# FFN weight halves made in the steps of pairs 3 to 5, the low ones on GpSimd, instead of in pairs 6 to 13 on VectorE

## The reference

```python
mod = silu(c) @ wmod                         # sa, ca, ga, sb, cb, gb for each sequence
h = layernorm(x) * (1 + ca) + sa
x = x + ga * linear_attention_with_memory(h) # 32 dims, causal
h = layernorm(x) * (1 + cb) + sb
gate = softmax(h @ w_gate.T); top 2 of 8 experts, weighted by cw
y = gelu(h @ W1[e] + b1[e]) @ W2[e] + b2[e]  # W1: 8 x 128 x 512, W2: 8 x 512 x 128
x = x + gb * sum over experts of cw * y
```

## Time and profile before

| | |
|---|---|
| median of 3 runs | 492.51 us (491.37 to 492.91) |
| the profiled execution's own time | 490.82 us |
| its span, first to last instruction | 489.0 us |
| VectorE busy | 417.5 us (85%) |
| TensorE busy (matmul) | 342.1 us (70%) |
| ScalarE busy | 306.5 us (63%) |
| GpSimd busy | 304.6 us (62%) |

### The profile page before, as it was taken

The page is one execution under the profiler, slowest core; times in us unless marked ns, Lnnn a source line. Parts: engine busy times, 40 slices in busy tenths (PEclk is TensorE's granted clock), DMA queues, the critical chain, the costliest instruction groups (busy, mean ns, idle before and its releaser), DMA issues.

```text
span 489.0 us, 13386 instructions
## 1 busy us (share of the span) xinstructions
PE 342.1 (70%) x3736; PEld 303.2 (62%) x3737; DVE 417.5 (85%) x1078; ACT 306.5 (63%) x691; POOL 304.6 (62%) x360
## 2 busy tenths in 40 slices
PE   1673664738765785673389999999999999995000
PEld 1462564627664665562269989999999999984000
DVE  1879999889998889885759888989899898988997
ACT  1262483739993998373166676776767677669930
POOL 2208830037774776576777834888888888887760
PEclk9976766958985888587599999999999999999555
DMA  8895000002420333235165564666655665653653
GB/s 211 216 312 207 3 1 0 7 22 99 145 102 33 135 104 109 69 97 167 53 173 149 146 117 111 143 145 141 148 137 141 145 145 137 143 122 95 180 157 107
DMA packets 98774, 59.62 MB, mean 122 GB/s; under 512 B 45872, under 2 KB 92080, under 8 KB 98480
## 3 DMA queue, kind: packets, MB, share of 16 engines
q1 hardware_dynamic: 90544, 42.38, 31.3%
q0 software_dynamic: 8192, 16.79, 13.3%
HBM read 21.75 MB, written 23.10 MB: 92 GB/s over the span
## 4 chain that ended last, share of the span: by engine, by line
PE 47%; DVE 34%; issue 9%; ACT 7%; DVEq 1%; ACTq 1%; POOL 0%; POOLq 0%
PE psA L1296 20%; PE psA L1284 10%; PE psV L1284 5%; PE psH L1284 5%; DVE ATT L812 3%; DVE stats L751 2%; PE psH L1182 2%; DVE X L1107 2%; DVE X L888 2%; DVE w_parts L1021 2%; DVE stats L895 1%; ACT ATT L649 1%; DVE ROW L1104 1%; PE psA L1191 1%; PE psA L1193 1%
## 5 line engine op out<-in xcount | busy, mean ns | idle before, releaser
L536 POOL DMA_INDIRECT expert_rows<-ROW,POS x128 | 130.6, 1020 | 71.4 <-issue 37.2
L1296 PE MATMUL psA<-WST,ATT 128*128 x1704 | 114.0, 220 | 1.7 <-DVE ATT L1077 1.7
L1296 PEld LDWEIGHTS psA<-WST,ATT 128*128 128x128 f16 x1704 | 103.2, 98 | 8.9 <-issue 2.8
L1077 DVE SCALAR_TENSOR_TENSOR ATT<-ATT,f_scales 128x1024 f16<-128x1024 f32 x71 | 91.2, 1284 | 2.5
L551 POOL DMA_INDIRECT ROW<-expert_out,POS x64 | 69.3, 1083 | 29.9 <-issue 26.6
L694 ACT ACTIVATE ATT<-psA,b1T,f_scales 128x256 f32<-128x256 f32 x144 | 69.6, 563 | 27.4 <-PE psA L1284 27.0
L551 POOL DMA_INDIRECT BIG<-expert_out,POS x64 | 67.6, 1056 | 17.7 <-issue 15.9
L1075 DVE TENSOR_SCALAR ATT<-ATT,f_scales 128x1024 f16<-128x1024 f32 x71 | 53.8, 757 | 7.2 <-ACT ATT L694 2.1
L1284 PE MATMUL psA<-WT,WST 128*128 128x256 f16 x432 | 54.4, 277 | 3.1 <-ACT ATT L694 1.6
L694 ACT ACTIVATE ATT<-psV,b1T,f_scales 128x256 f32<-128x256 f32 x70 | 35.7, 561 | 30.7 <-PE psH L1284 30.7
L1182 PE MATMUL psH<-ident,ATT 128*128 128x128 f32 x64 | 14.7, 371 | 47.9 <-DVE ATT L812 47.9
(11 more groups left out here) (246 smaller groups left out, 757.1 us busy)
## 6 DMA issues: line engine op xcount, KB each, us to landing
expert_out<-VP SPq DMA_DIRECT2D x71, 128.0 KB
X<-in_x SPq DMA_DIRECT2D x8, 512.0 KB, 7.0
WST<-in_W SPq DMA_DIRECT2D x2, 2048.0 KB, 14.6
WST<-WT SPq DMA_DIRECT2D x16, 256.0 KB
out<-X SPq DMA_DIRECT2D x15, 256.0 KB, 2.3
expert_rows<-ROW,POS POOLq DMA_INDIRECT x128
GA<-gate_rows SPq DMA_DIRECT2D x1, 2048.0 KB, 10.1
GA<-gate_rows SPq DMA_DIRECT2D x1, 1792.0 KB, 10.9
```

Of the source, the lines that this page charges most:

```text
L536: nc.gpsimd.indirect_dma_start(xg, bass.IndirectOffsetOnAxis(ap=POS[:, k * TILES + t:k * TILES + t + 1], axis=0), ROW[:, t * 2 * D:(t + 1) ...
L1077: nc.vector.scalar_tensor_tensor(out=GL[:, k % 2, :], in0=G[:, k % 2, :], scalar=f_scales[:, 3:4], in1=GH[:, k % 2, :], op0=ALU.mult, op1= ...
L1296: last = mm(psD[k % 2][:, h * D:(h + 1) * D], a[:, k % 2, i:i + TOK], W2S[:, ds(e * 2 * FF + b * FF + m * D, D)], start=(m == 0 and c == 0 ...
```

## The change

The weights' magnitudes are reduced earlier (`first_bound` and `middle_bounds` after step 1, `last_bound` beside step 2), the scales follow after step 2, and the statistics of the first layer norm that stood there move one step later each. The high halves are made by ScalarE in steps 3, 4 and 5 (5, 5 and 6 chunks). GpSimd makes the low halves with two instructions a chunk: it scales the f32 chunk in place and subtracts the high half. The halves go to a ring of four chunks in the part of `ROW` that is not yet written (instead of two in `WT`); ScalarE waits before chunk c until chunk c-4 has been moved by DMA, and before `route(0)` until all are moved. SyncE issues the moves of chunks 0 to 8 after `MR` of pair 5, 9 to 13 after that of pair 6, 14 and 15 after that of pair 7. VectorE's low halves are gone.

```diff
@@ -48,6 +48,8 @@
+    WRING = 4
+    WSTEP = {3: range(0, 5), 4: range(5, 10), 5: range(10, 2 * E)}
@@ -163,7 +165,7 @@
-        WP = WT[:].bitcast(f16).rearrange("p (i c) -> p i c", i=2)
+        WP = ROW[:, TILES * D:TILES * D + WRING * 2 * FF].rearrange("p (i c) -> p i c", i=WRING)
@@ -264,14 +267,15 @@
             for p in range(-1, 6):
-                step(p, p % 2, p // 2, bisect(PAIRS_TO, p - 2), **({"beside": beside[p]} if p in beside else {}))
+                step(p, p % 2, p // 2, bisect(PAIRS_TO, p - 2), **({"beside": beside[p]} if p in beside else {}),
+                     **({"weights": WSTEP[p]} if weights and p in WSTEP else {}))
...
-                        step(2 * n + k, k, n, g + 1, **({"weights": (g, 2 * n - 6 + k)} if weights else {}))
+                        step(2 * n + k, k, n, g + 1)
@@ -406,10 +410,8 @@
             def move(c):
-                if 0 <= c < 2 * E:
-                    for i in range(2):
-                        sp.wait_ge(ws_low, c + i + 1)
-                        sp.dma_start(WCHUNKS[:, (c + i) * FF:(c + i + 1) * FF], WT[:, i * FF:(i + 1) * FF]).then_inc(ws_moved[i], 16)
+                sp.wait_ge(ws_low, c + 1)
+                sp.dma_start(WCHUNKS[:, c * FF:(c + 1) * FF].bitcast(f16), WP[:, c % WRING, :]).then_inc(ws_moved[c % WRING], 16)
@@ -418,10 +420,11 @@
                 sp.dma_start(MR[:, p % 2, :], MEMO[:, p, :]).then_inc(mr_in[p % 2], 16)
-                move(2 * (p - LOOPED - 3))
+                for c in {5: range(0, 9), 6: range(9, 14), 7: range(14, 2 * E)}.get(p, ()):
+                    move(c)
@@ -464,9 +467,6 @@
-            for i in range(2):
-                nc.gpsimd.memset(WP[:, i, 0:1], 0.0).then_inc(ws_moved[i], 16)
@@ -522,6 +522,14 @@
             nc.gpsimd.partition_all_reduce(w_bound_all[:, 0:3], w_bound[:, 0:3], 128, bass.bass_isa.ReduceOp.max).then_inc(wb_all, 1)
+            pool.wait_ge(ws_ready, 4)
+            for c in range(2 * E):
+                chunk = WCHUNKS[:, c * FF:(c + 1) * FF]
+                pool.wait_ge(ws_high, c + 1)
+                nc.gpsimd.tensor_scalar(chunk, chunk, f_scales[:, c // E:c // E + 1], None, ALU.mult).then_inc(ws_scaled, 1)
+                pool.wait_ge(ws_scaled, c + 1)
+                nc.gpsimd.tensor_tensor(WP[:, c % WRING, FF:2 * FF], chunk, WP[:, c % WRING, 0:FF], ALU.subtract).then_inc(ws_low, 1)
@@ -576,13 +584,11 @@
-            def weights_high(pair, n):
-                c = 2 * pair
-                for i in range(2):
-                    ge(act, ws_moved[i], 16 * (pair + 1))
...
+            def weights_high(c):
+                ge(act, ws_moved[c % WRING], 16 * (c // WRING))
+                nc.scalar.activation(WP[:, c % WRING, 0:FF], WCHUNKS[:, c * FF:(c + 1) * FF], ACT.Copy,
+                                     scale=f_scales[:, c // E:c // E + 1]).then_inc(ws_high, 1)
@@ -625,7 +631,8 @@
                     act.wait_ge(ws_ready, 4)
-                    weights_high(weights[1], weights[0])
+                    for c in weights:
+                        weights_high(c)
@@ -677,13 +684,16 @@
             def route(g):
+                if g == 0:
+                    for i in range(WRING):
+                        act.wait_ge(ws_moved[i], 16 * 2 * E // WRING)
...
-            steps(act, step, route, {0: lambda: first_norm(1), 2: lambda: first_norm(2), 4: lambda: act.wait_ge(ln1_ready, 3)},
+            steps(act, step, route, {0: lambda: first_norm(1), 3: lambda: first_norm(2)},
                   weights=True, last=last_rows)
@@ -811,15 +821,7 @@
-            def weights_low(c, n):
-                for i in range(2):
-                    ge(dve, ws_high, c + i + 1)
-                    nc.vector.scalar_tensor_tensor(out=WP[:, i, FF:2 * FF], in0=WCHUNKS[:, ds((c + i) * FF, FF)],
...
@@ -871,8 +873,6 @@
-                if weights is not None:
-                    weights_low(2 * weights[1], weights[0])
@@ -1057,16 +1057,18 @@
-            def bounds_and_tiles():
+            def scales_and_bounds():
                 scales()
+                first_bound()
+                middle_bounds()
+            def weights_and_tiles():
+                weight_scales()
                 tiles(LN1[2], SECOND_HALF)
-            def last_refine():
-                refine(2)
-                middle_bounds()
-            steps(dve, step, route, {0: second_statistics, 1: bounds_and_tiles, 2: lambda: statistics(2, SECOND_HALF + BESIDE), 3: last_refine, 4: weight_scales},
-                  weights=True, beside={2: lambda: tiles(SECOND_HALF, SECOND_HALF + BESIDE), 3: first_bound, 4: last_bound})
+            steps(dve, step, route, {0: second_statistics, 1: scales_and_bounds, 2: weights_and_tiles,
+                                     3: lambda: statistics(2, SECOND_HALF + BESIDE), 4: lambda: refine(2)},
+                  beside={2: last_bound, 3: lambda: tiles(SECOND_HALF, SECOND_HALF + BESIDE)})
```

More of the change, by code:

```diff
@@ L214, in build_adaln_block @@
         bnd_ready, bnd_all, wb_ready, wb_all = sem("bnd_ready"), sem("bnd_all"), sem("wb_ready"), sem("wb_all")
-        ws_ready, ws_high, ws_low, ws_moved = sem("ws_ready"), sem("ws_high"), sem("ws_low"), [sem(f"ws_moved{i}") for i in range(2)]
+        ws_ready, ws_high, ws_low, ws_moved = sem("ws_ready"), sem("ws_high"), sem("ws_low"), [sem(f"ws_moved{i}") for i in range(WRING)]
+        ws_scaled = sem("ws_scaled")
         xn_ready, xn_turned, hT_ready = sem("xn_ready"), sem("xn_turned"), sem("hT_ready")
@@ L420, in _ @@
                 sp.dma_start(MR[:, p % 2, :], MEMO[:, p, :]).then_inc(mr_in[p % 2], 16)
-                move(2 * (p - LOOPED - 3))
-            for i in range(2):
-                sp.wait_ge(ws_moved[i], 16 * (E + 1))
+                for c in {5: range(0, 9), 6: range(9, 14), 7: range(14, 2 * E)}.get(p, ()):
+                    move(c)
+            for i in range(WRING):
+                sp.wait_ge(ws_moved[i], 16 * 2 * E // WRING)
             sp.wait_ge(zeroed, 16)
@@ L578, in _ @@
             nc.scalar.activation(gate_terms[:, 0:1], gate[:], ACT.Exp, scale=-1.0).then_inc(g_exp, 1)
-            def weights_high(pair, n):
-                c = 2 * pair
-                for i in range(2):
-                    ge(act, ws_moved[i], 16 * (pair + 1))
-                    nc.scalar.activation(WP[:, i, 0:FF], WCHUNKS[:, ds((c + i) * FF, FF)], ACT.Copy,
-                                         scale=f_scales[:, n:n + 1]).then_inc(ws_high, 1)
+            def weights_high(c):
+                ge(act, ws_moved[c % WRING], 16 * (c // WRING))
+                nc.scalar.activation(WP[:, c % WRING, 0:FF], WCHUNKS[:, c * FF:(c + 1) * FF], ACT.Copy,
+                                     scale=f_scales[:, c // E:c // E + 1]).then_inc(ws_high, 1)
             def rows(s):
@@ L812, in norm, with step @@
                 return nc.vector.tensor_scalar(out, x, mean, rstd, ALU.subtract, ALU.mult)
-            def weights_low(c, n):
-                for i in range(2):
-                    ge(dve, ws_high, c + i + 1)
-                    nc.vector.scalar_tensor_tensor(out=WP[:, i, FF:2 * FF], in0=WCHUNKS[:, ds((c + i) * FF, FF)],
-                                                   scalar=f_scales[:, n:n + 1], in1=WP[:, i, 0:FF], op0=ALU.mult,
-                                                   op1=ALU.subtract).then_inc(ws_low, 1)
-            def step(p, j, half, g, weights=None, beside=None):
+            def step(p, j, half, g, beside=None):
                 q, r = p - 1, p - 2
@@ L1311, in turn_needs @@
                 mm(psQK[0:1, 0:CHUNKS], need_col[:], ident[:, 0:CHUNKS], start=True, stop=True).then_inc(need_turned, 1)
-            for i in range(2):
-                pe.wait_ge(ws_moved[i], 16 * (E + 1))
+            for i in range(WRING):
+                pe.wait_ge(ws_moved[i], 16 * 2 * E // WRING)
             pe.wait_ge(row_ready, PAIRS)
```

## The result

The changed kernel takes 523.41 us (median of 6 runs, 523.06 to 524.14), the kernel before 491.55 (6 runs, 491.24 to 492.91): a ratio of 1.064, 95% interval 1.0623 to 1.0657. The forecast was 518 us in a range of 505 to 524, so the sign was right and the time lies at the range's upper edge. The profiled execution of the changed kernel took 524.14 us, its span 522.3. In its lines 843 has become 845, 812 is 822, 584 is 590 and 642 is 649; 881 has kept its number.

A forecast was written before the change was run, and what follows sets the result against it. TensorE and VectorE hold most of the chain; attention steps are bound by VectorE, then the path from `XN2` to `HL`. 490.8 + 1.7 + 0.7 + 11.7 + 17.8 - 6.1 = 516.6, forecast 518 us as the median, range 505 to 524.

The forecast's parts named there:

- Data and scales: Before step 3: VectorE waits 1.7 us for `b2B`, loses 0.7 of cover, waits 11.7 at the scales for GpSimd.
- No second load: Rival: GpSimd's second reduction loads no code, so the scales' wait is 5.9 instead of 11.7; 512 us, chance 0.29.
- The ring: Steps 3 to 5 and `route(0)`: waits for chunks' return through GpSimd and DMA cost 17.8 us, at 2.1 a chunk.
- The shared port: Steps 3 to 5: GpSimd may delay VectorE's `XN2` by 2 us, covered by ScalarE's ring wait; zero in the sum.
- VectorE pays the port, or the scaling costs 1.26: Rival: GpSimd blocks VectorE beyond the ring's cover, or scaling makes a chunk 2.7 us; 522 to 528 us, chance 0.07.
- The gain: Steps 6 to 13: without weight work each falls from 9.56 to 8.80 us, 6.1 in all (4.6 to 10.6).
- Not slower: Rival: the experts' first slot doesn't move with the steps, so early waits vanish; 492 us or less, chance 0.04.
- ring hides all: Rival: a chunk and its DMA fit within three high halves (2 us), ScalarE never waits; 500 us, chance 0.05.
- The signs of being wrong: GpSimd at the magnitudes before 62 us, a chunk clearly under 2 us, or step 6 under 20 us later than 106.2.

The follow-up runs named there:

- experiment 1: Kernel before with only VectorE's order of the changed kernel (earlier reductions and scales); halves still made in steps 6 to 13: 506.37 us, ratio 1.0259.
- experiment 7: Changed kernel with one more reduction over partitions on GpSimd behind the last chunk, its result unread: 528.58 us, ratio 1.0718.
- experiment 6: Changed kernel with GpSimd's small operations on the cells moved behind chunk 4 instead of ahead of the second reduction: 519.7 us, ratio 1.0546.
- experiment 3: Kernel before with one added GpSimd product behind the second reduction over partitions, its result unread: 485.57 us, ratio 0.9853.
- experiment 8: Changed kernel with eight ring places, ScalarE's wait for all moves at route 1, low halves on VectorE, one tiny GpSimd product: 504.92 us, ratio 1.0235.
- experiment 4: Changed kernel with eight ring places instead of four and ScalarE's wait for all moves at route 1 instead of route 0: 509.07 us, ratio 1.0327.
- experiment 2: Kernel before without making the halves in steps 6 to 13; the 16 moves stay and carry zeros from a GpSimd memset: 490.88 us, ratio 0.9964.
- experiment 5: Changed kernel without GpSimd's scaling instruction, so a chunk there is the subtraction alone: 514.85 us, ratio 1.0435.

## Why the prediction was right, and where it was not

The forecast case named the right places for the losses: the data, the scales behind a second load, the ring in steps 3 to 5 and the route. It did not have the head and put the port at nothing, and its sum came out near partly by luck, because errors of both signs met. In the order of its terms:

**Data and scales (1.7, 0.7, 11.7).** Right for the old head: 13.9 for 14.1 us in experiment 1. The changed kernel starts 6.6 us earlier on VectorE, which then stands at 42.6 for the same data, so the data's wait becomes 7.28; GpSimd's cells end 5 us earlier (61.9), so the scales' wait becomes 7.12. The step that failed was to leave the head as it was: the added chunks make GpSimd end on other code than it did, a gain that no term held. Step 3 starts at 73.18 us, for 76.52 in experiment 7 and 79.70 in experiment 1, so it is worth 3.3 to 6.5 us there.

**No second load (0.29).** It falls: 5.94 us here, 6.12 in experiment 6, 5.76 in experiment 7. The Trainium skill, "GPSIMD Engine Reference", section 2.1, speaks of a load of about 6 us at the first call to a freshly loaded kernel; the rows agree if each change of code counts as fresh, for the same reduction pays it at each of its two calls.

**The ring (17.8).** Mis-sized: against the order alone, steps 3, 4, 5 and route 0 grew by 5.5, 6.3, 9.9 and 4.9, together 26.6. The chunk: 2.8 for 2.1, since the scaling takes 1.57 us and not 0.65. The estimate put an operation with one input below one with two; here it is above it (1.15). GpSimd starts chunk 0 at 75.95 although its high half ended at 74.9, where in step 4 it follows within 0.1 us; chunk 4 waits 4.34, chunk 9 only 3.35. A third load, back from the reduction's code, lies behind the chunks' configuration at 68.2: experiments 3 and 8 show 6.70 and 6.89 us of it with no input missing, which would end near 75.1. The remaining 0.8 us before chunk 0 are not explained. `HL` lasts 1.43 to 1.50 instead of 0.69. In the route 2.5 were forecast and VectorE waits 4.93: the last two moves go out at 130.29, behind `MR` of pair 7, which hangs on a step that itself came later, and at the moment when GpSimd ends chunk 15.

**The shared port (nothing).** Wrong, though the rows named the suspect. For `XN2` nothing was right: its four operations take 1.11 us in each of steps 3 to 5. But `HL`, behind ScalarE's ring, is not covered by it: three times 0.7 to 0.8 us longer than the 0.69 of other steps, and two small operations are held by 0.4 and 0.7 us, together some 3.5 us. With the ring of eight the port matters more: in experiment 4 operations of 0.16 us last 1.1, all the lengthened ones together some 8 us more than in experiment 8, and experiment 8, which takes GpSimd away, gives 4.15 us back even after VectorE pays for the low halves itself. The Trainium skill, "SBUF — State Buffer", section "Who interferes with whom", has the second of such a pair blocked until the first is through; the row that ends 0.03 us behind the subtraction agrees, the 0.62 us beside the scaling do not. The rival *VectorE pays the port, or the scaling costs 1.26* (0.07) names a time that fits as well: 522 to 528 us, with its chunk of 2.7; it lacks the head too.

**The gain (6.1).** 2.55 in the changed kernel, 3.0 in the steps of experiment 2, 1.6 in its time; all below the 4.6 given as the worst. The step that failed is the choice of 8.80 for a step without weight work from steps 5, 14 and 15; the looped ones take 9.2.

**Not slower, ring hides all.** Neither happened. The delay in front of step 6, 35.3 us, less 2.55 is 32.7, and the span grew by 33.3: nothing was absorbed.

**The signs of being wrong.** By the letter one came true: GpSimd was to reach the magnitudes not before 62 us, and its cells end at 61.92. The reduction then begins at 67.86, near the 67 that were given for no load, and yet the load is there: the earlier head had moved all of it forward by some 5 us, and only the idle time in front of the row tells the two cases apart. Steps 6 to 13 take 9.24, outside the 8.5 to 9 given.

Put together, by VectorE's starts: 15.2 (order, step 6 of experiment 1) - 6.5 (head, step 3 against experiment 1) + 26.6 (ring, chunks, port) - 2.6 (gain) = 32.7 us. The first three add up by construction to the delay of step 6; the span grew by 33.3 and the median by 31.9. The forecast had 14.1, 0, 17.8 and 6.1, 25.8 in all: too little by 1.1, 8.8 and 3.5, too much by the 6.5 of the head. With the old head (experiment 7) the time is 528.6, outside the range even without the 1 us of its series.

## What to carry to other kernels

Before moving work to an engine that sits idle, read the wait that the work would hide in where it is: VectorE's low halves cost little, because VectorE waits for `HH` anyway, and taking them out, together with ScalarE's high ones, gave 3 us in eight steps. A wait in an in-order queue costs everything queued behind it, and a return path through two engines and a transfer has to be counted again in every part once one part gets faster: with GpSimd's share more than halved (experiment 5), the route waited as long as before, now for SyncE's order alone. Look at GpSimd's idle time behind each configuration, at the head of the program too: which code GpSimd held last decides what the next execution pays, and one instruction in an idle place was worth 1.5%.

## What the runs showed of the hardware that was not expected

What GpSimd ran last is kept from one execution to the next. Memsets and indirect DMAs apart: where the reduction over partitions is its last operation, the next execution idles 8.8 to 9.1 us ahead of its first operation (the kernel before, experiments 1, 2 and 7); where a product, a scaling or a subtraction comes behind it, 0.65 (the changed kernel, experiments 3 to 6 and 8). Memsets and indirect DMAs don't count: all these programs end on such instructions, the first memsets of the kernel before run at 0.3 us, ahead of the idle time, and experiment 2's memset of 128 x 2048 starts right behind the reduction, with no gap (85.69 us), and leaves its head late (9.37). A scaling by a column, 128 x 512 in place, takes GpSimd 1.57 us, longer than the subtraction of two tensors of that size (1.15). An operation of VectorE that is held beside the subtraction ends with it, one beside the scaling is held for a part of it (experiment 4: 1.10 and 0.62 us instead of 0.16); not every one is held: the four of line 888 take 1.12 us beside a subtraction there, as in experiment 8. And GpSimd is held as well: the scaling that starts at 84.31 in the changed kernel, while `HL` runs until 84.87, lasts 2.00 instead of 1.57 us.
